# Edge network of a two-layer graph kernel: rows made unique over a pair of tiles, the pair's accumulating scatters issued back to back

## The chip, the cores and the metric

The kernel runs on one core of a Trainium2 chip, in one launch. The metric is the device time of that launch in microseconds (us), as the median of several runs. Engines are named as in the profile: PE is TensorE (PEld its weight loads), DVE is VectorE, ACT is ScalarE, POOL is GpSimd, SP is SyncE.

## What is computed

50000 nodes with 256 features, 50000 edges (`src`, `dst`, sorted by `dst`). A graph attention layer and a layer norm come first; then the edge network, which the change touches; then a last layer norm. Cut to the edge network:

```python
h = jnp.concatenate([n_embed[senders], n_embed[receivers]], axis=-1)   # senders = src
h = jnp.tanh(h @ W0 + b0)
h = jnp.tanh(h @ W1 + b1)
h = h @ W2 + b2
h = h * (e_embed @ Wg)
m = _segment_mean(h, senders, n)
out = _layernorm(x + m)
```

`segment_mean` adds the edge rows that have the same sender and divides by their count.

## The kernel before, in words

The kernel is a sequence of stages. The stage before the edge network writes two tables to HBM: PA (406 columns of the receiver or sender half of `h @ W0`, with the reciprocal count beside it, 408 columns in all) and PB (the other half), and the array x, which is `out_x`. The edge network (from L1269 on) then takes the edges in 98 groups of four tiles of 128 edges, and two groups' buffers alternate (index `s`). The last stage (L1656 on) is the layer norm over `out_x`.

What each engine does for group g of the edge network:

- POOL `gather` (L1311): two indirect DMAs per tile bring 128 rows of PA and of PB into `u_pa` and `u_pb`; eight per group. `scatter` (L1324): one indirect DMA per tile adds the 128 summed rows in `u_sums` to `out_x` in HBM at the rows in `u_row`; four per group. Rows out of bounds are dropped. `body` (L1340) gathers group g+2 and scatters group g-2 in turns. A scatter waits until the evacuation of its half group and its row numbers are there, and until all earlier scatters have landed (`need(pool, o_st, 16 * (4 * g + j))`, L1328), since two tiles can hold the same sender and an accumulating DMA reads, adds and writes.
- DVE `add` (L1550): waits for the eight gathers, copies the reciprocal counts (L1554) and adds PA to PB (L1555, L1559). `low0`, `low1`, `edge_low`, `low_message` make the low parts of numbers that are split in two for the f32r products. `message` multiplies layer 2 by the gate. `select` (L1584) builds for each tile the 128x128 matrix that sums rows of equal key inside the tile into the first of them, and counts in `u_first` how many of the rows up to itself have a row's key; `scatter_rows` (L1593) moves rows that are not the first beyond the bound.
- PE: `transposes` of the summed rows for group g+1, `layer1`, `gate`, `layer2` of group g, `combine` (L1414: the selection times the high and the low message, a pair of tiles per half of one PSUM bank), `spread` (the keys as a row for `select`).
- ACT: tanh twice per product (`hidden0`, `hidden1`), `gated`, `high_message`, and `sums` (L1502), which evacuates the bank of `combine` to `u_sums`.

Each engine runs its own list in program order, written out by hand; semaphores tie them. In its body for group g the DVE ends with `add(g + 2)`, and the body for g+1 begins with `select(g)`. In the PE's body for group g+1 the first thing behind `layer1(g+1, 0)` is `transposes(g+2, 0)`, which needs that `add`.

```python
def free(g):                       # POOL, ahead of a group's gathers
    pool.wait_ge(v_ix, g + 1)
    need(pool, v_sum, g - 1)
    need(pool, p_t, 4 * (g - 1))
```

Where the kernel's last two groups have no gathers beside them, POOL issues scatters alone: 16 of them, behind the last one that had gathers ahead of it.

## Time and profile before

| | us |
|---|---|
| median of three runs (lowest, highest) | 6148.02 (6139.2, 6167.52) |
| the profiled execution, its own time | 6160.46 |
| its span in the trace | 6158.8 |
| the edge network's POOL instructions, first to last start | 3787.04 to 5831.44 |
| busy in the span: PE, DVE, ACT, POOL | 4460.0 (72%), 3805.1 (62%), 2758.8 (45%), 3465.6 (56%) |

The page cuts the span into 40 slices of 154 us. The edge network fills the slices from the 25th to the 38th; the last one or two belong to the layer norm. In these slices PE and POOL both show seven or eight tenths, the DVE and ACT six, the DMA engines five. A line of the timeline gives the start, the duration, the engine and the source line, and in brackets how long the engine had stood idle before and what ended that: "issue" means that nothing shown in the profile was waited for.

### The profile page before, as it was taken

What the parts mean: (1) busy time and instruction counts of PE and PEld (TensorE: products, weight loads), DVE (VectorE), ACT (ScalarE), POOL (GpSimd) and SP (SyncE); (2) the same over time, 40 slices, a digit from 0 to 9 for tenths busy, and PEclk for the clock granted to TensorE, in tenths of its full rate; (3) what the DMA queues carried; (4) which work ended last, traced back from release to release, by engine and by line L of the source; (5) the groups of instructions that cost most, each with busy time, mean ns of one, the idle gap of its engine ahead of it and who ended that gap; (6) DMA issues with size and microseconds to landing.
All of it is one profiled execution on the core that took longest, in us unless ns stands there. A gap on an engine that the chain in (4) does not pass through costs nothing. (4 is left out here: it accounts for less than half of the span.)

```text
span 6158.8 us, 98689 instructions
## 1 busy us (share of the span) xinstructions
PE 4460.0 (72%) x23300; PEld 3492.5 (57%) x23300; DVE 3805.1 (62%) x12481; ACT 2758.8 (45%) x6177; POOL 3465.6 (56%) x3119
## 2 busy tenths in 40 slices
PE   7998555555555556649999997888888888888500
PEld 6776222222222334439999996777777777777400
DVE  5666555555554455559898985665656656565364
ACT  1222222222222233326666664666666666666365
POOL 1112555555555566645555554777777777777422
PEclk9999666666676677779999998999999999999755
DMA  5664000000000655559999996555555555555397
GB/s 163 201 201 133 7 6 6 6 6 6 6 7 5 145 158 169 158 156 365 356 370 359 368 355 219 122 121 122 122 120 119 123 121 120 120 122 121 58 376 290
DMA packets 721257, 940.50 MB, mean 153 GB/s; under 512 B 179231, under 2 KB 632856, under 8 KB 708704
## 3 DMA queue, kind: packets, MB, share of 16 engines
q0 software_dynamic: 183840, 376.08, 27.1%
q10 hardware_dynamic: 216893, 321.19, 14.5%
q1 hardware_dynamic: 320471, 242.66, 12.3%
q8 instruction: 16, 0.26, 0.0%
q14 instruction: 37, 0.30, 0.0%
HBM read 514.78 MB, written 425.15 MB: 153 GB/s over the span
## 5 line engine op out<-in xcount | busy, mean ns | idle before, releaser
L1189 PE MATMUL bank<-w0r,n_x1T 128*128 128x406 f32 x4704 | 903.8, 351 | 34.2 <-ACT n_pa L1237 18.4
L1189 PEld LDWEIGHTS bank<-w0r,n_x1T 128*128 128x128 f32 x4704 | 868.9, 189 | 57.8 <-ACT n_pa L1237 40.2
L1330 POOL DMA_INDIRECT out_x<-u_sums,u_row x392 | 673.3, 1718 | 238.9 <-issue 178.1
L576 PE MATMUL bank<-table,ohloT 128*128 128x392 f32 x784 | 484.8, 710 | 412.2 <-issue 208.3
L1383 PE MATMUL bank<-u_h,w1r 128*108 128x512 f32 (+1 forms) x2646 | 749.5, 432 | 0.0
L520 POOL DMA_INDIRECT DS<-by_dst,rank_int x392 | 387.9, 990 | 540.1 <-DVE by_dst L635 427.3
L1383 PEld LDWEIGHTS bank<-u_h,w1r 128*108 128x108 f32 (+1 forms) x2646 | 476.2, 187 | 144.9
L681 POOL DMA_INDIRECT xg<-XP,m_src x392 | 415.1, 1059 | 246.3 <-DVE m_src L697 126.1
L1065 POOL DMA_INDIRECT n_cg<-CT,n_last x392 | 445.3, 1136 | 177.0 <-issue 95.1
L1313 POOL DMA_INDIRECT u_pa<-PA,u_rows x392 | 441.1, 1125 | 170.5 <-issue 103.9
L1313 POOL DMA_INDIRECT u_pb<-PB,u_rows x392 | 436.1, 1113 | 119.5 <-issue 119.5
L1383 PE MATMUL bank<-w2r,u_h 108*128 108x256 f32 x3528 | 480.8, 281 | 0.2 <-DVE u_h L1574 0.2
L576 PEld LDWEIGHTS bank<-table,ohloT 128*128 128x128 f32 x784 | 167.4, 251 | 552.2 <-ACT ohloT L550 295.2
L621 DVE CUSTOM_DVE_ANT_0 found<-bank,ohhi,earlier 128x392 f32<-128x392 f32 x392 | 242.9, 620 | 382.5 <-remote 293.0
L1371 PE MATMUL bank<-ident,u_pb 128*128 128x128 f32 (+1 forms) x1568 | 258.6, 291 | 265.5 <-DVE u_pb L1559 264.9
L528 POOL DMA_INDIRECT r_sgather<-XP,r_dst x392 | 378.9, 967 | 126.3 <-issue 118.2
L1383 PEld LDWEIGHTS bank<-w2r,u_h 108*128 108x128 f32 x3528 | 444.2, 188 | 0.4 <-DVE u_h L1574 0.4
L784 PE MATMUL bank<-msg,m_sel 128*128 128x260 f32 x784 | 272.0, 506 | 208.4 <-DVE msg L731 170.9
L550 ACT CAST ohloT<-bank 128x128 f32<-128x128 f16 x392 | 104.4, 266 | 676.0 <-remote 408.3
L1371 PEld LDWEIGHTS bank<-ident,u_pb 128*128 128x128 f32 (+1 forms) x1568 | 195.8, 144 | 342.2 <-issue 163.2
L328 DVE TENSOR_SCALAR ohhi<-iota,key_hi 128x392 f16<-128x392 f16 x1176 | 381.7, 325 | 1.0 <-issue 1.0
L1475 ACT ACTIVATE u_tanh_k<-bank,b0s 128x512 f32<-128x512 f32 (+1 forms) x392 | 272.1, 694 | 223.5 <-PE bank L1371 211.6
(258 smaller groups left out, 10221.4 us busy)
## 6 DMA issues: line engine op xcount, KB each, us to landing
PA<-n_pa ACTq DMA_DIRECT2D x98, 816.0 KB
PB<-n_pb ACTq DMA_DIRECT2D x98, 812.0 KB
XP<-xps POOLq DMA_DIRECT2D x98, 528.0 KB, 4.1
CT<-ct ACTq DMA_DIRECT2D x98, 528.0 KB
n_xp<-XP SPq DMA_DIRECT2D x98, 528.0 KB
xin<-in_x SPq DMA_DIRECT2D x97, 512.0 KB, 4.9
n_x<-in_x SPq DMA_DIRECT2D x97, 512.0 KB
out_x<-n_x ACTq DMA_DIRECT2D x97, 512.0 KB, 5.1
```

The costliest lines, as they stand in the source:

```text
L328: o = nc.vector.tensor_scalar(ohhi[q][s][:, j, :], iota[:, 0:NT], HI[q][:, t], None, ALU.is_equal)
L520: pool.indirect_dma_start(out=DS, out_offset=bass.IndirectOffsetOnAxis(ap=ri[s][:, j:j + 1], axis=0), in_=pd[s][:, j, :], in_offset=None). ...
L528: pool.indirect_dma_start(out=sg[s][:, j, :], out_offset=None, in_=XP, element_offset=D + HEADS, in_offset=bass.IndirectOffsetOnAxis(ap=ix ...
L576: nc.tensor.matmul(B[ub[b]][:, 0:NT], oT[b][:], tab[b][:], start=True, stop=True)\
L681: pool.indirect_dma_start(out=xg[r][:, j, :], out_offset=None, in_=XP, in_offset=bass.IndirectOffsetOnAxis(ap=sr[r][:, j:j + 1], axis=0))\
L1065: pool.indirect_dma_start(out=cg[s][:, j, :], out_offset=None, in_=CT, in_offset=bass.IndirectOffsetOnAxis(ap=il[s][:, j:j + 1], axis=0)). ...
L1189: o = nc.tensor.matmul(acc, xT[s][p][:, k, e], w0r[q][:, 2 * half + k, :], start=(n == 0), stop=(n == len(terms) - 1))
L1313: pool.indirect_dma_start(out=buf[s][:, j, 0:w], out_offset=None, in_=table, in_offset=bass.IndirectOffsetOnAxis(ap=ix[s][:, 1 - q, j:j + ...
L1330: pool.indirect_dma_start(out=out, out_offset=bass.IndirectOffsetOnAxis(ap=si[s][:, j:j + 1], axis=0), in_=yo[s][:, j, :], in_offset=None, ...
L1371: o = nc.tensor.transpose(TB[k % 2][0:n, j * P:(j + 1) * P], pb[s][:, j, a:a + n], ident[:])
L1383: o = nc.tensor.matmul(acc, a[p], b[q], start=(start and n == 0), stop=(stop and n == 2))
L1475: nc.scalar.activation(thk[k % 2][0:n, :], TB[k % 2][0:n, :], ACT.Tanh, bias=b0s[0:n, k:k + 1])
```

## The change

The four tiles of a group become two pairs. Within a pair (a, b) the selection is built over both tiles: tile a's matrix now also gets the rows of b that have the same key as a row of a, and a row of b counts as the first of its key only if neither a nor the rows of b before it hold the key. So the two tiles of a pair never add to the same row.

- `select`: for each pair one operation of 128x128 as before (tile a) and one of 128x256 (the keys of a and b against those of b), with the new constant `u_prior` (ones beside the triangle `upto`), set up once before the first group.
- `combine`: six products per pair where there were four: a with a, and b into a (accumulated), and b with b.
- `scatter` waits for the landing of earlier scatters only at the even tile.
- POOL's body issues four gathers, then the pair's two scatters, and so again.

```diff
-            sel = alloc(ph, "u_sel", [P, G, P], f32r)
+            sel = alloc(ph, "u_sel", [P, G // 2, 3, P], f32r)
+            prior = alloc(ph, "u_prior", [P, 2 * P])
...
-                        need(pool, o_st, 16 * (4 * g + j))
+                        if j % 2 == 0:
+                            need(pool, o_st, 16 * (4 * g + j))
...
-                        for j in range(G):
-                            if not late(g, 2):
-                                gather(s, j)
-                            if not early(g, 2):
-                                scatter(g - 2, s, j)
+                        for h in range(G // 2):
+                            for j in (2 * h, 2 * h + 1):
+                                if not late(g, 2):
+                                    gather(s, j)
+                            for j in (2 * h, 2 * h + 1):
+                                if not early(g, 2):
+                                    scatter(g - 2, s, j)
...
-                        for j in (2 * h, 2 * h + 1):
-                            acc = CB[:, (j % 2) * D:(j % 2 + 1) * D]
-                            for q in range(2):
-                                o = nc.tensor.matmul(acc, sel[:, j, :], mg[s][q][:, j, :], start=(q == 0), stop=(q == 1))
+                        a, b = 2 * h, 2 * h + 1
+                        terms = [(0, 0, a, q) for q in range(2)] + [(0, 1, b, q) for q in range(2)]
+                        terms += [(1, 2, b, q) for q in range(2)]
+                        for n, (k, m, j, q) in enumerate(terms):
+                            o = nc.tensor.matmul(CB[:, k * D:(k + 1) * D], sel[:, h, m, :], mg[s][q][:, j, :],
+                                                 start=(n in (0, 4)), stop=(n in (3, 5)))
...
+                    c.did(nc.vector.memset(prior[:, 0:P], 1.0))
+                    c.did(nc.vector.tensor_copy(prior[:, P:2 * P], upto[:]))
...
-                        for j in range(G):
-                            o = nc.vector.scalar_tensor_tensor(sel[:, j, :], TB[1][:, j * P:(j + 1) * P], kf[s][:, j:j + 1],
-                                                               upto[:], ALU.is_equal, ALU.mult, accum_out=cnt[s][:, j:j + 1])
+                        for h in range(G // 2):
+                            a, b = 2 * h, 2 * h + 1
+                            nc.vector.scalar_tensor_tensor(sel[:, h, 0, :], TB[1][:, a * P:b * P], kf[s][:, a:a + 1],
+                                                           upto[:], ALU.is_equal, ALU.mult, accum_out=cnt[s][:, a:a + 1])
+                            o = nc.vector.scalar_tensor_tensor(sel[:, h, 1:3, :].rearrange("p m n -> p (m n)"),
+                                                               TB[1][:, a * P:(b + 1) * P], kf[s][:, b:b + 1], prior[:],
+                                                               ALU.is_equal, ALU.mult, accum_out=cnt[s][:, b:b + 1])
```

POOL's list before, one body ahead of the loop, with the semaphores that an instruction waits for. `u_out_added` counts landed scatters, `u_evacuated` is the evacuation by ACT, `u_transposed` and `u_sum` say that a group's buffers are free again:

```order
L1313 DMA u_pa<-PA,u_rows 128x408 [waits u_transposed,u_rows,u_sum]
L1313 DMA u_pb<-PB,u_rows 128x406
L1330 DMA out_x<-u_sums,u_row 50000x256 [waits u_out_added,u_evacuated,u_scatter_rows]
L1313 DMA u_pa<-PA,u_rows 128x408
L1313 DMA u_pb<-PB,u_rows 128x406
L1330 DMA out_x<-u_sums,u_row 50000x256 [waits u_out_added,u_evacuated,u_scatter_rows]
```

The same body after the change; the line numbers have moved by one or two:

```order
L1314 DMA u_pa<-PA,u_rows 128x408 [waits u_transposed,u_rows,u_sum]
L1314 DMA u_pb<-PB,u_rows 128x406
L1314 DMA u_pa<-PA,u_rows 128x408
L1314 DMA u_pb<-PB,u_rows 128x406
L1332 DMA out_x<-u_sums,u_row 50000x256 [waits u_out_added,u_evacuated,u_scatter_rows]
L1332 DMA out_x<-u_sums,u_row 50000x256 [waits u_evacuated,u_scatter_rows]
```

Two gathers and a scatter, four times, have become four gathers and two scatters, twice; the second scatter of a pair no longer waits for `u_out_added`.

The DVE's list around `select` before, from the end of one body to the first low parts of the next:

```order
L1554 COPY u_rc<-u_pa 128x4 [waits u_gate,u_gathered0]
L1555 TENSOR_TENSOR u_pb<-u_pb,u_pa 128x4x3x22
L1559 TENSOR_TENSOR u_pb<-u_pb,u_pa 128x4x384
L1589 SCALAR_TENSOR_TENSOR u_sel,u_first<-bank,u_key,upto 128x128 [waits u_combined,u_keys_spread]
L1589 SCALAR_TENSOR_TENSOR u_sel,u_first<-bank,u_key,upto 128x128 x3
L1574 TENSOR_TENSOR u_h<-u_tanh_m,u_h 108x512 [waits u_tanh_m]
```

and after:

```order
L1562 COPY u_rc<-u_pa 128x4 [waits u_gate,u_gathered0]
L1563 TENSOR_TENSOR u_pb<-u_pb,u_pa 128x4x3x22
L1567 TENSOR_TENSOR u_pb<-u_pb,u_pa 128x4x384
L1598 SCALAR_TENSOR_TENSOR u_sel,u_first<-bank,u_key,upto 128x128 [waits u_combined,u_keys_spread]
L1600 SCALAR_TENSOR_TENSOR u_sel,u_first<-bank,u_key,u_prior 128x256
L1598 SCALAR_TENSOR_TENSOR u_sel,u_first<-bank,u_key,upto 128x128
L1600 SCALAR_TENSOR_TENSOR u_sel,u_first<-bank,u_key,u_prior 128x256
L1582 TENSOR_TENSOR u_h<-u_tanh_m,u_h 108x512 [waits u_tanh_m]
```

The number of operations is the same; every second one is twice as wide.

## Rows read from the trace of the kernel before

**Rows 1.** Timeline of POOL, first gather of the first body with scatters. Columns: start us, us, engine, line, operation, tiles, count, idle before.
```profile
3848.44 0.95 POOL L1313 DMA_INDIRECT u_pa<-PA,u_rows  x1 [11.38 <-PE bank L1371]
```

**Rows 2.** Groups of POOL, 4000 to 5500 us: count | busy us, mean ns | idle before.
```profile
L1330 POOL DMA_INDIRECT out_x<-u_sums,u_row x296 | 509.4, 1721 | 148.3 <-issue 142.1 <-DMA out_x<-u_sums,u_row 6.3
L1313 POOL DMA_INDIRECT u_pa<-PA,u_rows x296 | 331.9, 1121 | 90.2 <-issue 78.9 <-DVE u_row L1599 8.2 <-ACT u_sums L1506 3.1
L1313 POOL DMA_INDIRECT u_pb<-PB,u_rows x296 | 331.7, 1121 | 90.2 <-issue 90.2
```

**Rows 3.** Timeline of POOL, the turn from one group to the next.
```profile
4510.85 0.99 POOL L1313 DMA_INDIRECT u_pa<-PA,u_rows  x1 [0.30 <-ACT u_sums L1506]
4512.14 1.05 POOL L1313 DMA_INDIRECT u_pb<-PB,u_rows  x1 [0.30 <-issue]
4513.91 1.71 POOL L1330 DMA_INDIRECT out_x<-u_sums,u_row  x1 [0.72 <-issue]
4515.92 2.54 POOL L1313 DMA_INDIRECT u_pa<-PA,u_rows  x1 [0.31 <-issue]
4518.77 1.35 POOL L1313 DMA_INDIRECT u_pb<-PB,u_rows  x1 [0.30 <-issue]
```

**Rows 4.** Timeline of DVE, the same turn and two operations ahead of it.
```profile
4511.59 0.42 DVE L1604 TENSOR_TENSOR u_message<-bank,u_gate 128x256 f32<-128x256 f32 x1
4511.93 0.42 DVE L1608 TENSOR_TENSOR u_msg<-u_message,u_msg 128x256 fp32r<-128x256 f32 x1
...
4515.43 0.17 DVE L1554 COPY u_rc<-u_pa 128x4 f32<-128x4 f32 x1 [0.75 <-DMA u_pb<-PB,u_rows]
4515.86 1.75 DVE L1559 TENSOR_TENSOR u_pb<-u_pb,u_pa 128x1536 f32<-128x1536 f32 x1
4517.52 0.34 DVE L1589 SCALAR_TENSOR_TENSOR u_sel<-bank,u_key,upto 128x128 fp32r<-128x128 f32 x1
4518.61 0.69 DVE L1574 TENSOR_TENSOR u_h<-u_tanh_m,u_h 108x512 fp32r<-108x512 f32 x1
4520.41 0.21 DVE L1598 TENSOR_SCALAR u_first<-u_first 128x4 f32<-128x4 f32 x1
```

**Rows 5.** Timeline of PE, the same turn, and the `combine` ahead of it.
```profile
4504.25 0.71 PE L1422 MATMUL bank<-u_msg,u_sel 128*128 128x256 f32 x4
4504.80 0.60 PE L1371 MATMUL bank<-ident,u_pb 128*86 128x128 f32 x4
...
4517.66 0.66 PE L1371 MATMUL bank<-ident,u_pb 128*128 128x128 f32 x4 [2.41 <-DVE u_pb L1559]
4518.07 3.69 PE L1383 MATMUL bank<-u_h,w1r 128*108 128x512 f32 x9
```

**Rows 6.** Waits from 4000 to 5500 us: total us, times, longest.
```profile
PE bank L1371 <- DVE u_pb L1559: 186.3, 74, 4.7
...
DVE u_rc L1554 <- DMA u_pb<-PB,u_rows: 80.0, 42, 3.4
```

**Rows 7.** Timeline of PE early in the stage, where the DVE does not wait for gathers.
```profile
3913.58 0.66 PE L1371 MATMUL bank<-ident,u_pb 128*128 128x128 f32 x4 [1.33 <-DVE u_pb L1559]
...
3931.94 0.65 PE L1371 MATMUL bank<-ident,u_pb 128*128 128x128 f32 x4 [1.49 <-DVE u_pb L1559]
3932.35 2.33 PE L1383 MATMUL bank<-u_h,w1r 128*108 128x512 f32 x9
```

**Rows 8.** A stretch: us, busy of PE, PEld, DVE, ACT, POOL, PEclk, DMA share, GB/s.
```profile
4074.90:4078.00 3.10, 3.10 (x10) 2.22 (x9) 1.83 (x7) 1.27 (x2) 2.58 (x2) 0.50 0.37 74
```

**Rows 9.** Timeline of POOL, the end of the stage: no gathers any more from 5754.68 on.
```profile
5754.68 1.71 POOL L1330 DMA_INDIRECT out_x<-u_sums,u_row  x1 [0.61 <-issue]
5759.56 1.57 POOL L1330 DMA_INDIRECT out_x<-u_sums,u_row  x1 [3.16 <-DMA out_x<-u_sums,u_row]
...
5831.44 1.55 POOL L1330 DMA_INDIRECT out_x<-u_sums,u_row  x1 [2.93 <-DMA out_x<-u_sums,u_row]
```

**Rows 10.** DMA queues from 5800 to 5830 us, where only scatters run.
```profile
q0 software_dynamic: 1004, 0.87, 26.2%
```

## The prediction

> **What bounds the kernel now.** I read the page's slices first: the edge network is the longest stage and its POOL and PE rows are equally high, so shares decide nothing. The groups of POOL inside the steady stretch come next. In 1500 us POOL issued 296 scatters of 1.721 us and 592 gathers of 1.121 us; its idle time was 148.3 us ahead of the scatters and 180.4 us ahead of the gathers [rows 2]. That adds up to 1501.8 us: POOL is never without work. The reader is to see what the idle time is. A gather costs 90.2 / 296 = 0.305 us of it, always, which is the gap between any two of these instructions. A scatter has 148.3 / 296 = 0.501 us, so 0.196 us more. That excess is the wait for the scatter before to land: where scatters run alone, the next one starts 3.17 us after the end of the one before (5754.68 + 1.71 to 5759.56) [rows 9], and two undisturbed gathers with three gaps are only 0.99 + 1.05 + 0.91 = 2.95 us [rows 3].
>
> A group is 296 / 4 = 74 to the 1500 us, 20.3 us; over the whole stage it is the same, (5756.4 - 3848.4) / 94 = 20.30 us for the 94 bodies that have gathers and scatters [rows 1, 9]. Written out: 8 x (1.121 + 0.305) + 4 x (1.721 + 0.501) = 20.3.
>
> PE is the follower. It waits 186.3 / 74 = 2.5 us per group for the DVE's addition, and the DVE waits 80.0 / 74 = 1.08 us per group for the gathers to land [rows 6]. How fast the chain of PE, ACT and DVE could go by itself is seen early in the stage, where the DVE does not wait for gathers: from one transposition to the next 18.36 us, with 1.3 to 1.5 us of waiting in front of it [rows 7]. So there are two clocks: POOL at 20.3 us and the compute chain at 18.4 us.
>
> **POOL's holds.** In the turn between two groups a gather took 2.54 us instead of 0.99 [rows 3]. It started at 4515.92, just behind the DVE's long addition (4515.86 to 4517.61) [rows 4], and ended 0.85 us after it: it was held until the addition was over. The next one started inside the DVE's low part (4518.61 to 4519.30) [rows 4] and took 1.35 us. Undisturbed a gather is 0.97 us and a scatter 1.62 [rows 3], so the means of rows 2 hold 8 x 0.15 + 4 x 0.10 = 1.6 us per group of such holds.
> The Trainium skill, "SBUF — State Buffer", section "Who interferes with whom", says that one of the DVE and GpSimd takes the shared port pair for a whole instruction and the other blocks, but it adds, marked as inferred, that a tensor_tensor takes only the read interface while descriptor generation needs the write interface. By that addition these holds would be zero and POOL's group 18.7 us today; the rows show 20.3, so here the measurement decides, and POOL's starts are held by tensor_tensor operations whose inputs both lie in SBUF.
>
> **The change part by part.**
> - The wait between scatters. The odd scatter waits for nothing but POOL itself; the even one for a scatter whose issue ended four gathers earlier, 5 x 0.305 + 4 x 0.97 = 5.4 us, against 3.17 us to land [rows 9]. Both waits go: 4 x 0.196 = 0.78 us per group. 20.30 becomes 19.5 us.
> - The holds. Counted from the end of a group's last gather (4513.19), the DVE resumed at +2.24 and its long addition began at +2.67 [rows 3, 4]. Before, one scatter lay between and the next gather started at +2.73, into the addition. Now two scatters follow: the second starts at +0.31 + 1.62 + 0.31 = +2.24, ahead of the addition, and runs until +3.9; the next gather starts at +4.2 and the addition ends at +4.4. So of the hold of 1.55 us some 0.2 remains where the phases are as in this turn. Where the DVE comes later (it sometimes has no wait for gathers), the first gather is held by up to 1.2 us. Bounds: the holds fall from 1.6 to some 0.9 us, or rise by 0.4. I take a fall of 0.3, nearer to no change than to the one favourable turn: POOL at 19.2 us.
> - PE. Two more products per pair. Four took 4504.25 to 4504.80, 0.14 us each [rows 5], so 4 x 0.14 = 0.55 us per group, wholly on the compute chain, which becomes 18.36 + 0.55 = 18.9 us. It lies beside POOL as long as POOL needs more than that. This is the floor of the change.
> - DVE. The four selections take 4517.52 to 4518.61, 0.27 us each. A product of 128x256 out of PSUM takes 0.34 us from start to start (4511.59 to 4511.93) [rows 4]. So a selection twice as wide adds between 0.34 - 0.27 = 0.07 and, if all of it goes by width, 0.27 us; two of them per group 0.14 to 0.54 us. I take 0.27. While they run, PE is in nine products of layer 1 that need nothing of them (4518.07 to 4521.76) [rows 5], so they are covered, and if that cover goes they cost their 0.27 us on the chain.
> - The two setup operations on the DVE run once, before the first gathers have landed: nothing.
> - The end. After the last gathers 16 more scatters ran, until 5831.44 + 1.55 = 5832.99, 76.6 us behind 5756.39 [rows 9]. Now they are 8 pairs of 1.55 + 0.31 + 1.55 + 3.17 = 6.6 us; the last ends 8 x 6.6 = 52.6 us behind. That is 24 us less. Behind the last gathers the compute chain has two groups left, 2 x 18.9 = 38 us, and the seventh pair wants the last group's sums at 3.2 + 6 x 6.6 = 43 us; so POOL stays the limit there.
>
> Sum: 94 x (20.3 - 19.2) = 103 us, and 24 us at the end: 127 us. From the profiled execution's 6160.5 that is 6033; the median of the runs lies 12.4 us lower than that execution, so the prediction against the median is **6021 us**.
>
> **Rivals.**
> 1. The compute chain becomes the bound. If the holds fall to 0.9 us, POOL would go at 18.8 us and the chain's 18.9 decides. The DVE's waits for gathers then vanish, and POOL waits ahead of a group's first gather for the transpositions. 94 x 1.4 + 24 = 156: 5992 us. For it speaks the phase above; against it, that the phase of one turn is not that of all. Chance 0.27.
> 2. The holds stay or grow: POOL at 19.5 to 19.9 us, 94 x 0.8 or 0.4, with the end 99 or 62 us: 6049 to 6086 us. Chance 0.2 (in most of it still over 0.5% faster, which is 31 us, about what a measurement of this kernel can tell from no change).
> 3. The PE's clock takes the gain back. Behind its long waits the granted clock was 0.50, that is 1.2 of 2.4 GHz [rows 8], and the nine products of layer 1 took 3.69 us instead of 2.33 [rows 5, 7], 1.36 us. A chain of 18.9 + 1.4 = 20.3 us would leave only the end: 6124 us. Against it: once the chain is late, PE's wait is down to 1.3 to 1.5 us, and behind such a wait the products took 2.33 [rows 7]; so the lower clock cannot hold in every group. Chance 0.07.
> 4. Slower: the pair lands late. Two accumulating scatters in a row could take the engines so long that the second lands well beyond 3.17 us. POOL's next pair waits once it exceeds the 5.4 us of cover, two times per group, and each microsecond beyond costs 2 us in a group. Nothing is gained any more at about 5.4 + (0.78 + 0.26) / 2 = 5.9 us, and at 6.3, two landings one after the other, it is 94 x (19.5 + 1.8 - 20.3) = 94 us slower in the bodies and nothing saved at the end: 6242 us. Already from about 6 us the DVE too would stand at `scatter_rows` (4520.41, that is +7.2) [rows 4], with low parts queued behind it that PE needs. Against it: the scatters running alone filled 26.2% of the DMA engines at one per 4.7 us [rows 10], 1.2 us each, less than the 1.92 us that POOL needs for the next. Chance 0.06.
>
> **How the numbers follow.** Forecast (POOL at 19.1 to 19.4) 0.4, rivals 1 to 4 as given. The range takes in the first three up to the top of rival 2 and leaves out rivals 3 and 4 and a rest at the low edge: 5980 to 6085 us. Faster by over 0.5% is the forecast, rival 1 and nearly all of rival 2: 0.86. Within 0.5% is rival 3 and the edge of 2: 0.08. Slower is rival 4: 0.06.
>
> **What would show it.** Idle ahead of both scatters of a pair 0.30 to 0.31 us in the steady stretch; the mean of a gather below 1.121 us and few gathers above 2 us; six products per half group in `combine`; the DVE's wait for gathers clearly below 1.08 us per group, and PE's below 2.5. Rival 1 shows as POOL idle behind PE at the first gather of groups, and no DVE wait for DMA; rival 3 as layer 1 at 3.3 to 4.2 us in most groups; rival 4 as POOL idle "by DMA out_x" at even scatters. I am wrong if POOL still stands idle longer than 0.31 us at scatters, if the second scatter's own duration exceeds 1.7 us on the mean, or if PE's waits grow.

## The result and the profile after

Where it was first measured, the changed kernel took 6293.7 us (median of four runs, 6279.8 to 6310.6) and the kernel before 6150.2 us (four runs here, three in the table of before): ratio 1.0232, 95% interval 1.0196 to 1.0268. It is **slower by 2.3%**; that it is slower is clear of the noise, that it is so by more than 2% just isn't. The prediction (6021 us, 5980 to 6085) missed it in size and in sign. The profiled execution has a span of 6278.1 us at a mean granted clock of 0.835 (before: 6158.8 and 0.844).

The experiments ran later and mostly on other chips, and this can't be left out: the kernel before takes 5636 to 5655 us on four of them (numbers 5, 7, 14 and 9) and 6210 us on a fifth (number 6), which behaves as the first one did. The first chip's number isn't on record, so it may be number 6 itself. On chip 7 the changed kernel is **faster by 3.2%**. The rest of this text is about what lies between the two results. Ratios below are always taken on one chip; times per group are also compared across the four chips of 5650 us, on which the kernel before agrees within 0.4%.

The groups of POOL in the changed kernel on the first chip, 4000 to 5500 us (count | busy us, mean ns | idle before), which answer to [rows 2]:

```profile
L1332 POOL DMA_INDIRECT out_x<-u_sums,u_row x274 | 457.5, 1670 | 83.5 <-issue 82.9 <-DVE u_rows L1556 0.6
L1314 POOL DMA_INDIRECT u_pa<-PA,u_rows x275 | 347.1, 1262 | 248.4 <-PE bank L1375 172.1 <-issue 76.3
L1314 POOL DMA_INDIRECT u_pb<-PB,u_rows x275 | 279.9, 1018 | 85.0 <-issue 74.4 <-DMA out_x<-u_sums,u_row 10.1 <-DVE u_rows L1556 0.6
```

The wait that the change takes away is gone: 83.5 / 274 = 0.305 us ahead of a scatter, the bare gap, instead of 0.501. But a group is now 4 x 1500 / 274 = 21.9 us, and POOL stands 172.1 us behind PE's transpositions, of which [rows 2] have nothing. The waits of the same stretch (us in total, times, longest), which answer to [rows 6]:

```profile
PE bank L1375 <- DVE u_pb L1567: 195.7, 68, 4.5
ACT u_gate L1500 <- PE bank L1387: 177.9, 121, 2.9
POOL u_pa L1314 <- PE bank L1375: 172.1, 46, 5.9
...
ACT u_gate L1500 <- remote: 48.0, 21, 3.1
```

PE waits 195.7 / 68 = 2.9 us each time for VectorE's addition, no less than before, and a releaser stands here that the same stretch of the kernel before does not have: "remote", a wait that ended with no instruction of this core. The timeline of the same kernel shows what it looks like (start us, us, engine, line, operation, tiles, count, idle before):

```profile
4543.75 1.23 PE L1387 MATMUL bank<-w2r,u_h 108*128 108x256 f32 x9
...
4545.48 1.22 PE L1387 MATMUL bank<-w2r,u_h 108*128 108x256 f32 x9
4545.58 1.67 POOL L1332 DMA_INDIRECT out_x<-u_sums,u_row  x1 [0.30 <-issue]
...
4546.53 0.60 PE L1435 MATMUL bank<-ident,u_key 128*128 128x128 f32 x4
4546.89 2.31 PE L1387 MATMUL bank<-u_h,w1r 128*108 128x512 f32 x9
4547.55 1.58 POOL L1332 DMA_INDIRECT out_x<-u_sums,u_row  x1 [0.30 <-issue]
4548.34 0.48 ACT L1500 ACTIVATE u_gate<-bank,u_rc 128x256 f32<-128x256 f32 x1 [3.05 <-remote]
...
4553.24 1.11 PE L1375 MATMUL bank<-ident,u_pb 128*128 128x128 f32 x4 [3.80 <-DVE u_pb L1567]
4554.01 4.19 PE L1387 MATMUL bank<-u_h,w1r 128*108 128x512 f32 x9
```

PE's layer 2 of tile 2 ended at 4544.98, and ScalarE's gate, whose other condition (the message of tile 0) was long met, began at 4548.34: by the trace the product was done 3.4 us before ScalarE could act on it. The trace models the ends of products, but PE had by then begun three later groups of products (at 4545.48, 4546.53 and 4546.89). Message, low part, the next addition all follow, PE waits 3.8 us at its end, and layer 1 behind that wait takes 4.19 us instead of 2.33 [rows 7], on the lower clock: the granted clock from 4553.3 to 4558.2 us is 0.50, which is 1.2 of 2.4 GHz.

How often this happens can be counted over the whole stage, from the starts and ends of the 392 layers 2 and the 392 gates, wherever ScalarE stood idle ahead of the gate. In the changed kernel 147 of 260 such gates began over 0.3 us after the end of their product, by up to 4.16 us and by 1.06 us on the mean of the 260. In the kernel before it is 33 of 280, by up to 1.78 and by 0.14 us on the mean. In the changed kernel on chip 7 it is none of 287, and the longest is 0.04 us. "Late" and "on time" below mean this. From ScalarE to VectorE (gate to message) and back (message to its cast) no start is more than 0.04 us behind its releaser, on the first chip as on the others, and on the four chips of 5650 us TensorE's signals aren't late either. The trace's own records of semaphores can't give these counts on the first chip: it holds 322 of the 392 signals of layer 2 there.

The changed kernel on chip 7, 3500 to 5000 us, first POOL's groups:

```profile
L1332 POOL DMA_INDIRECT out_x<-u_sums,u_row x325 | 521.9, 1606 | 99.0 <-issue 99.0
L1314 POOL DMA_INDIRECT u_pa<-PA,u_rows x325 | 357.8, 1101 | 99.1 <-issue 99.1
L1314 POOL DMA_INDIRECT u_pb<-PB,u_rows x325 | 325.7, 1002 | 99.1 <-issue 99.1
```

then one of its stretches (us, busy of PE, PEld, DVE, ACT, POOL, PEclk, DMA share, GB/s):

```profile
4000.00:4500.00 500.00, 457.77 (x3085) 397.49 (x3086) 339.24 (x847) 352.43 (x677) 400.95 (x326) 1.00 0.65 133
```

Here POOL has no wait of any kind, only gaps of 0.305 us; a group is 6000 / 325 = 18.5 us, and TensorE's granted clock is 1.00.

### The profile page after: what moved, and what is told of

Its sections match the earlier page's. It is cut to its first block and busy times, and to the rows that moved or that the text cites. A ratio compares the mean times of both kernels' runs of the same rounds, so it can differ in the third digit from the quotient of the medians.

```text
span 6278.1 us, 99187 instructions
## 1 busy us (share of the span) xinstructions
PE 4561.4 (73%) x23692; PEld 3588.4 (57%) x23692; DVE 3833.3 (61%) x12483; ACT 2755.9 (44%) x6177; POOL 3460.3 (55%) x3119
## 5 line engine op out<-in xcount | busy, mean ns | idle before, releaser
L1387 PE MATMUL bank<-u_h,w1r 128*108 128x512 f32 (+1 forms) x2646 | 813.0, 460 | 0.0
L1332 POOL DMA_INDIRECT out_x<-u_sums,u_row x392 | 653.4, 1667 | 147.0 <-issue 116.1
L1314 POOL DMA_INDIRECT u_pa<-PA,u_rows x392 | 489.0, 1247 | 392.1 <-PE bank L1375 245.8
L1387 PEld LDWEIGHTS bank<-u_h,w1r 128*108 128x108 f32 (+1 forms) x2646 | 508.6, 200 | 160.5
L1314 POOL DMA_INDIRECT u_pb<-PB,u_rows x392 | 399.1, 1018 | 120.9 <-issue 106.9
L1375 PEld LDWEIGHTS bank<-ident,u_pb 128*128 128x128 f32 (+1 forms) x1568 | 210.6, 153 | 388.1 <-issue 230.6
L1582 DVE TENSOR_TENSOR u_h<-u_tanh_m,u_h 108x512 fp32r<-108x512 f32 (+1 forms) x294 | 203.3, 691 | 341.5 <-ACT u_h L1490 224.7
```

The lines of the kernel that those rows point to most:

```text
L1314: pool.indirect_dma_start(out=buf[s][:, j, 0:w], out_offset=None, in_=table, in_offset=bass.IndirectOffsetOnAxis(ap=ix[s][:, 1 - q, j:j + ...
L1332: pool.indirect_dma_start(out=out, out_offset=bass.IndirectOffsetOnAxis(ap=si[s][:, j:j + 1], axis=0), in_=yo[s][:, j, :], in_offset=None, ...
L1375: o = nc.tensor.transpose(TB[k % 2][0:n, j * P:(j + 1) * P], pb[s][:, j, a:a + n], ident[:])
L1387: o = nc.tensor.matmul(acc, a[p], b[q], start=(start and n == 0), stop=(stop and n == 2))
```

## The experiments

Time per group is 6000 / (number of scatters in 1500 us) all through, from 3500 to 5000 us on the chips of 5650 us and from 4000 to 5500 us on the other two. "The gates" are ScalarE's `gated`, which waits for PE's layer 2.

### The order and the wait apart (chip 5, kernel before 5648 us)

Gather and scatter by turns as before, with the halved waits:

```diff
-                        for h in range(G // 2):
-                            for j in (2 * h, 2 * h + 1):
-                                if not late(g, 2):
-                                    gather(s, j)
-                            for j in (2 * h, 2 * h + 1):
-                                if not early(g, 2):
-                                    scatter(g - 2, s, j)
+                        for j in range(G):
+                            if not late(g, 2):
+                                gather(s, j)
+                            if not early(g, 2):
+                                scatter(g - 2, s, j)
```

> The changed kernel with one thing put back: POOL issues gather, scatter, gather, scatter as before (two gathers, one scatter of one tile each time), the waits on the earlier scatter stay halved, selection and combination stay over the pair. Theory A (the order is what hurts: four gathers in a row on POOL delay when TensorE's results are seen by ScalarE, and the compute chain runs at 21.8 us per group): with the runs broken up the group falls to 19.2 to 19.9 us, 6030 to 6110 us in all. Theory B (the wider selection and the two more products per pair are what hurts, with TensorE's lower clock): the order changes nothing, 6270 to 6310 us.

Measured: 5565.0 us, ratio 0.9854 (0.9836 to 0.9871), 306 scatters in 1500 us, 19.6 us per group. The times that were expected here and of the next three kernels took the first chip's 6150 us for granted and are void; the times per group can be compared. 19.6 us seemed to fit theory A (the order hurts by late signals), but no signal is late on this chip, so the run doesn't bear on it.

The same edit the other way round, the pair order in the kernel before:

> The kernel before with one thing changed: POOL issues four gathers, then two scatters, each scatter still waiting for the one before it; selection and combination by the tile as before. Theory A (order hurts): the group takes 21 us or more without any added compute, 6220 to 6320 us. Theory B (added compute hurts): the second scatter of a pair now shows its full wait of some 3 us on POOL, which the gathers no longer cover, so POOL takes 4 us more per group at most if nothing absorbs it (up to 6500 us); its compute chain stays at 18.4 us. The two are told apart by where the waits are: ScalarE's gate waiting long after the end of TensorE's second layer under A, POOL without any wait for TensorE under B.

Measured: 5993.4 us, ratio 1.0612 (1.0594 to 1.0630), 23.9 us per group. Its groups of POOL:

```profile
L1330 POOL DMA_INDIRECT out_x<-u_sums,u_row x251 | 404.3, 1611 | 427.5 <-DMA out_x<-u_sums,u_row 289.4 <-DVE u_pb L1561 99.7 <-issue 38.4
```

This is theory B's arithmetic for POOL: a scatter waits 427.5 / 251 = 1.70 us on the mean, that is 0.3 for one of a pair and 3.1 for the other. That arithmetic holds whatever the added compute costs, so it doesn't show theory B itself. No gate is late. So the pair order alone, with all four waits, costs 3.6 us per group (20.3 to 23.9).

The wide selection alone, order and waits of before (`if j % 2 == 0:` taken out, and the diff above):

> The changed selection and combination over the pair alone: POOL's order and all four waits on the earlier scatter as before. Theory A: POOL still sets the pace as before, the added 0.55 us of TensorE and 0.27 us of VectorE per group are mostly hidden: 6140 to 6200 us. Theory B: 6270 to 6310 us, as the changed kernel.

Measured: 5630.2 us, ratio 0.9971 (0.9962 to 0.9981), 299 scatters, 20.1 us per group: the added products and the wider selections cost nothing here, where POOL sets the pace.

The changed kernel with `if j % 2 == 0:` alone taken out:

> The changed kernel with the wait of every second scatter put back: four gathers, two scatters, the second waits until the first has landed (about 3 us on POOL, twice a group). Theory A: the gathers still run four in a row, so it is no faster than the changed kernel: 6290 us and up, to 6500 if POOL becomes the bound again by the two waits (19.2 + 2 x 1.6 us per group is 22.4, 6340 us). Theory B: the same POOL arithmetic, so this run tells the two apart only by the gate's waits; it prices the wait itself.

Measured: 5990.7 us, ratio 1.0608 (1.0590 to 1.0626), 251 scatters, 23.9 us per group where 22.4 was expected, as `tile_pairorder` to 3 us. In this order the halved wait is worth 5.4 us per group (23.9 to 18.5), in the old order 0.5 (20.1 to 19.6).

### The changed kernel again (chip 7, kernel before 5655 us)

> The changed kernel itself, timed again beside the kernel before. What is asked: whether it is slower wherever it runs. The first measurement (6294 against 6150 us) shows ScalarE's gates starting up to 3 us after the end of the TensorE products that they wait for, put down to no instruction of the core; the four kernels timed since show none of this, and their kernel before took 5648 us. Theory A1 (the late signals are what made the changed kernel slower, and they belong to the place where it ran): where the kernel before takes 5650 us, the changed kernel has no late gates and takes 5560 to 5650 us. Theory A2 (the order of POOL's work costs time by itself, as the pair order with all waits does at 23.8 us per group): 5700 to 5990 us wherever it runs.

Measured: 5470.3 us, ratio 0.9677 (0.9657 to 0.9698). A2 falls. A1 has the direction right and misses in size: it expected 5560 to 5650 us. What the run shows is that late signals and the slower result go together; that the one makes the other is asked below. The version between, a second time:

> The changed kernel with POOL's order of before (gather, scatter by turns) and the halved waits, a second time. Where the kernel before takes 5650 us: 5565 us as the first time, 1.5% below. Where the kernel before takes 6150 us and gates start late: between 6030 and 6110 us if it is the runs of four gathers that the late signals follow, 6200 us and more if the shorter waits alone bring them.

Measured: 5563.3 us, ratio 0.9835 (0.9811 to 0.9858). The pair order is 93 us better than the order by turns once the wait inside a pair is gone. What either does where signals come late was only asked of the changed kernel.

### Lateness put in by hand (chip 14, kernel before 5636 us)

First the kernel before, for its trace:

> The kernel before itself, for its trace where it takes 5650 us. Theory L (late TensorE signals hit the changed kernel and spared the one before): the edge stage is the same as in the first trace, 20.1 to 20.4 us per group and some 76 us from the last gather to the end of the scatters, with no wait put down to anything but an instruction of this core; the 500 us lie ahead of the edge stage. Theory M (the place is simply faster): every stage is shorter, the edge stage too.

Measured: 5636.9 us, 296 scatters in 1500 us: the same 20.3 us per group as on the first chip. The first gather of the edge stage, on this chip and on the first:

```profile
3270.95 1.02 POOL L1313 DMA_INDIRECT u_pa<-PA,u_rows  x1 [33.48 <-DVE u_rows L1548]
```

```profile
3787.04 1.02 POOL L1313 DMA_INDIRECT u_pa<-PA,u_rows  x1 [33.53 <-DVE u_rows L1548]
```

516 of the 524 us between the two executions lie ahead of it. The waits of the kernel before on the first chip in one stretch of that part, 1200 to 1700 us, where POOL issues indirect transfers as well:

```profile
ACT ohloT L550 <- remote: 126.3, 32, 7.2
DVE found L621 <- remote: 111.9, 31, 6.0
...
ACT table L548 <- remote: 85.7, 29, 4.0
```

On chip 14 the part has no wait of that name. Theory L holds: the late signals were in the first trace before the change, mostly in another stage.

Then ScalarE is held up behind its wait for layer 2, in the changed kernel and in the one before (the new buffer `held` and its clearing are left out here; the double dose has two copies in place of one):

```diff
                         need(act, v_mf, 4 * g + j - 1)
+                        for k in range(1 if j else 0):
+                            nc.scalar.copy(held[:, 1 + 1 * (j % 2) + k, :], held[:, 0, :])
```

> The changed kernel with ScalarE held up for one copy of 128x512 (about 0.6 us) ahead of each of the gates of tiles 1 to 3, behind the wait for TensorE's layer 2: 1.8 us per group, as much as the gates waited longer in the first trace of the changed kernel. Theory L: the compute chain takes the pace from POOL and grows by most of it, 19.6 to 20.6 us per group instead of 18.5, 5570 to 5670 us. Theory N (the lateness of the gates is no cause, something else lengthened the group by 3.3 us): no more than 18.8 us per group, under 5510 us.

> The same with two such copies each, 3.6 us per group. Theory L: 21.3 to 22.6 us per group, the first measurement's 21.8, 5730 to 5860 us. Theory N: under 19.5 us per group, under 5570 us.

> The kernel before with the one copy ahead of the gates of tiles 1 to 3, 1.8 us per group. Theory L: its POOL sets 20.2 us per group and its compute chain of some 18.4 has 1.8 us of room, so nearly all of it is covered: 5640 to 5700 us, while the changed kernel with the same copies loses 100 to 200 us. If the kernel before has no such room: 5750 us and more.

Measured: `after_gate1` 5643.5 us (1.0016, 1.0006 to 1.0025), `after_gate2` 5645.7 us (1.0014, 1.0004 to 1.0023), `before_gate1` 5630.9 us (0.9993, 0.9982 to 1.0005). The changed kernel goes from 18.5 to 20.5 us per group (293 scatters) and loses all of its gain; the one before stays at 20.2 (297), its time just under the 5640 to 5700 us expected. The single dose is as theory L has it. The double dose isn't: 20.5 us lies above theory N's 19.5 and below theory L's 21.3 to 22.6. No hold-up on a chip with signals on time made the changed kernel slower than the one before by anything like 2%. The timelines of PE show why the two doses cost the same. `after_gate1`:

```profile
4512.81 0.66 PE L1376 MATMUL bank<-ident,u_pb 128*128 128x128 f32 x4 [1.78 <-DVE u_pb L1571]
4513.22 3.53 PE L1388 MATMUL bank<-u_h,w1r 128*108 128x512 f32 x9
...
4533.59 0.66 PE L1376 MATMUL bank<-ident,u_pb 128*128 128x128 f32 x4 [1.89 <-DVE u_pb L1571]
4533.99 3.79 PE L1388 MATMUL bank<-u_h,w1r 128*108 128x512 f32 x9
```

and `after_gate2`:

```profile
4516.41 0.66 PE L1376 MATMUL bank<-ident,u_pb 128*128 128x128 f32 x4 [2.46 <-DVE u_pb L1571]
4516.83 2.33 PE L1388 MATMUL bank<-u_h,w1r 128*108 128x512 f32 x9
```

with one stretch of each:

```profile
4000.00:4500.00 500.00, 451.42 (x2772) 380.87 (x2771) 305.57 (x763) 352.96 (x681) 386.28 (x293) 0.93 0.56 120
```

```profile
4000.00:4500.00 500.00, 421.54 (x2766) 360.97 (x2765) 304.92 (x763) 387.86 (x754) 384.94 (x293) 0.99 0.56 119
```

With the small dose layer 1 takes 3.4 to 3.9 us in 59 of the 67 groups that can be read there (the two shown have granted clocks of 0.61 and 0.56); with the large one it takes 2.33 in 62 of 70, and 3.2 to 3.3 in the other 8. Two different sums come to the same 20.5 us.

### The clock, and the chain by itself (chip 7, kernel before 5650 us)

Five idle products of 128x256 ahead of PE's wait for the addition keep it busy in the gap:

```diff
                         if k == 0:
-                            pe.wait_ge(v_sum, g + 1)
-                        if k == 0:
                             need(pe, v_e, g)
+                            for _ in range(5):
+                                nc.tensor.matmul(TB[0][:, 0:D], wgr[0][:, 0:P], wgr[0][:], start=True, stop=True)
+                            pe.wait_ge(v_sum, g + 1)
```

> The changed kernel with the 0.6 us copies ahead of the gates of tiles 1 to 3 (20.5 us per group, clock 0.93, 5643 us), and in addition five idle products of 128x256 on TensorE ahead of its wait for VectorE's add, where it stood still for 1.8 us per group; their result is overwritten. Theory C (most of the 2.0 us that the copies cost is TensorE at its lower clock behind that wait): the granted clock returns to 0.98 or more and the group to 18.6 to 19.3 us, 5480 to 5550 us. Theory D (the delay itself is what costs): the clock may return, the group stays at 20 us or above, 5600 us and more.

> The changed kernel with the five idle products alone. POOL sets 18.5 us per group and the clock is 1.00 already, so under both theories nothing is won: 5465 to 5480 us. If the products come in the way of the real ones (TensorE has about 1.6 us of idle time per group, they take some 1.4), up to 5530 us.

Measured: `after_gate1_fill` 5525.3 us (0.9786, 0.9762 to 0.9810) where the version without the idle products had a ratio of 1.0016; `after_fill` 5470.8 us (0.9686, 0.9663 to 0.9709), no loss. The turn in `after_gate1_fill`:

```profile
4519.28 0.75 PE L1368 MATMUL bank<-wgr 128*128 128x256 f32 x5
4521.23 0.66 PE L1377 MATMUL bank<-ident,u_pb 128*128 128x128 f32 x4 [1.20 <-DVE u_pb L1572]
4521.64 2.33 PE L1389 MATMUL bank<-u_h,w1r 128*108 128x512 f32 x9
```

Theory C holds: 19.1 us per group (314 scatters), so of the 2.0 us that the hold-up had cost, 1.4 came with the lower clock. The other 0.6 isn't the compute chain: POOL waits for nothing here either, as its first group shows, and its gathers have grown from 1.05 to (385.6 + 316.2) / 630 = 1.11 us on the mean:

```profile
L1315 POOL DMA_INDIRECT u_pa<-PA,u_rows x315 | 385.6, 1224 | 96.0 <-issue 96.0
```

So POOL sets the pace at 19.1 us as well, and the chain with the 1.9 us of copies and the full clock takes no more than that.

Then the scatters of the odd tiles are left out (with the counts that wait for them halved), so that POOL is no bound:

```diff
                     def scatter(g, s, j):
 
+                        if j % 2:
+                            return
```

> The changed kernel without the scatters of every second tile: half of the edges' sums are left out of the result, and POOL has 3.8 us less per group (about 14.7 us). What is left is the compute chain of the pair version. By the prediction's third step it takes 18.9 us per group; since the changed kernel runs at 18.5 with TensorE waiting 1.6 us per group, it must be below that: 17.5 to 18.4 us.

> The kernel before without the scatters of every second tile, again with half of the sums left out: the compute chain of the tile version. The prediction has it 0.55 us per group below the pair version (two products more per pair). If TensorE's added products stand beside another engine's work, as the equal times of the pair order with all waits at either width suggest, the two are within 0.2 us.

Measured: 165 scatters of two tiles each in 1500 us in both kernels, 18.2 us per group (5430.5 and 5433.6 us). The wait that ends last is now POOL's for PE, in the changed version:

```profile
POOL u_pa L1314 <- PE bank L1377: 221.0, 83, 2.7
```

The chain that is left is the same 18.2 us for the pair as for the tile, one run of each: the two added products per pair lie beside other work.

### Equal lateness in both (chip 9, kernel before 5646 us)

> The kernel before with two copies (1.2 us) ahead of each of the gates of tiles 1 to 3, 3.6 us per group. The changed kernel took 20.5 us per group and 5646 us with the same. Theory E (at equal lateness the two are level, since the compute chain is the same 18.2 us in both, so the first result needs more lateness in the changed kernel than in the one before): 20.3 to 21.0 us per group, 5640 to 5710 us. Theory F (the kernel before has some room of its own that the changed one lacks, so that equal lateness already makes the changed one slower): 20.1 us per group and under 5640 us.

> The version with POOL's order of before and halved waits (19.6 us per group, 5565 us), with one copy ahead of each of the gates of tiles 1 to 3. If the chain with these copies and TensorE's lower clock takes 20.5 us whatever POOL does: 20.4 to 20.6 us per group, 5625 to 5650 us. If the lower clock comes only with the changed kernel's order: 19.6 to 19.9 us per group, 5560 to 5590 us.

Measured: `before_gate2` 5673.2 us (1.0049, 1.0033 to 1.0064), 293 scatters, 20.5 us per group; `alt_even_gate1` 5647.5 us (1.0007, 0.9995 to 1.0019), 294 scatters, 20.4 us. Both come out as theory E and the first alternative had them, and none of the three versions is slower by 2% at equal lateness. That all three run at the pace of one chain isn't shown, though. In `alt_even_gate1` POOL stands 165.2 us of 1500 behind PE and in `after_gate2` 71.7, but in `before_gate2` it waits for PE almost never:

```profile
L1314 POOL DMA_INDIRECT u_pa<-PA,u_rows x293 | 356.1, 1215 | 91.5 <-issue 87.2 <-PE bank L1372 2.8 <-DVE u_row L1603 0.9
```

There POOL still sets the pace, with somewhat longer gathers, so the equal 20.5 us is in part a coincidence. What the runs do show is that equal lateness of the gates doesn't give the first result. That needs signals that are later in the changed kernel than in the one before, or late signals of other kinds beside the gates'.

### The same hold-ups on a chip with late signals (chip 6, kernel before 6210 us)

The last two kernels add a hold-up of VectorE ahead of the selection. They ran on a chip that has late signals of its own:

```diff
                         dve.wait_ge(p_m, g + 1)
+                        for k in range(2):
+                            nc.vector.tensor_tensor(held[:, 3 + k, :], held[:, 0, :], held[:, 0, :], ALU.subtract)
```

> The changed kernel with one copy (0.6 us) ahead of each of the gates of tiles 1 to 3, and VectorE held up for two subtractions of 128x512 (1.4 us) behind its wait for the spread keys. If lateness of both kinds is what made the first trace: 21.3 to 22.3 us per group at a clock of about 0.90, 5720 to 5820 us. If VectorE has room at that place: 20.5 us as without, 5645 us.

> The same two hold-ups in the kernel before (20.1 us per group and 5631 us with the gates' alone). If equal lateness brings both kernels to the pace of the same compute chain: within 0.5% of the changed kernel with the same hold-ups. If the kernel before has room of its own: under 20.6 us per group, under 5670 us.

Measured: `after_gate1_select` 6487.9 us, ratio 1.0441 (1.0406 to 1.0476), 257 scatters, 23.3 us per group; `before_gate1_select` 6226.7 us, ratio 1.0023 (1.0006 to 1.0041), 295 scatters, 20.3 us. The expectations in absolute time are void, since they assumed a kernel before of 5650 us. The comparison is not, and it was missed: expected within 0.5%, with the same hold-ups on the same chip the two are 4.2% apart, while chips 14 and 9 left them level. The copy that stands in front of the gate shows the difference in its idle time, first in the changed version, then in the one before, then in `after_gate1` on chip 14:

```profile
L1502 ACT COPY u_held<-u_held 128x512 f32<-128x512 f32 x193 | 119.9, 621 | 216.1 <-PE bank L1388 187.1 <-remote 26.8 <-issue 2.2
```

```profile
L1496 ACT COPY u_held<-u_held 128x512 f32<-128x512 f32 x223 | 138.5, 621 | 50.2 <-PE bank L1384 39.0
```

```profile
L1502 ACT COPY u_held<-u_held 128x512 f32<-128x512 f32 x222 | 138.4, 623 | 71.2 <-PE bank L1388 71.2
```

ScalarE waits for layer 2 1.12 us each time in the changed version, 0.23 in the one before and 0.32 where no signal is late. Where ScalarE stood idle ahead of the copy or the gate, 173 of 235 starts are over 0.3 us behind their product in the changed version, and 39 of 133 in the one before. The spread keys are late too: of their signals that the trace recorded 93 of 96 come over 0.1 us after the product in the changed version, 15 of 69 in the one before. The first chip had 147 of 260 and 33 of 280 gates. So **the lateness belongs to the chip that a kernel ran on, and its amount follows the kernel**: it is small with POOL's work by turns and large with the pair version. Each of the two measurements with late signals was taken at one time, so a chip can't be told from the time at which it was used; and the changed kernel without hold-ups was measured beside late signals on the first chip alone.

Since the pair order with all four waits (`pair_all`) and the order by turns with halved waits (`alt_even`) were never on such a chip, no run tells which of the two parts, the order or the missing wait, does it. The traces point to the order. Take the same starts of gates or copies and ask what POOL was issuing when the product ended. In the changed kernel on the first chip, 100 of 103 are late where that was the fourth gather in a row or the scatter behind it, 40 of 93 where it was the third gather, and 7 of 54 where it was the second. On chip 6, with the hold-ups, it is 118 of 120 (and 15 of 15 in the second scatter), 40 of 46 and 0 of 47. The kernel before never issues more than two gathers in a row; of its products that end in the first of them 0 of 68 are late on the first chip, and 32 of 202 of those that end in the second or in the scatter behind it (3 of 28 and 35 of 98 on chip 6). But the place in POOL's list goes with the tile whose product it is, so this is a sign and no test.

## Why the prediction was wrong, by its own steps

- **The wait between scatters** was right: 0.305 us ahead of each, on both kinds of chip.
- **The holds** were mis-sized, to the good side. On chip 7 a gather takes (357.8 + 325.7) / 650 = 1.05 us and a scatter 1.61, so by the undisturbed 0.97 and 1.62 the holds are 8 x 0.08 = 0.7 us per group; they fell by 0.9, not by 0.3. The long holds are gone, as in the favourable turn of [rows 3, 4]: 23 of 591 gathers take over 2 us in the kernel before on chip 14, 1 of 650 in the changed kernel on chip 7. POOL goes at 18.5 us, not at 19.2.
- **PE's 0.55 us on the chain** was wrong: it is zero (18.2 us with either width, one run each). The floor of 18.9 that rival 1 is built on does not exist.
- **The selections** were right: 0.476 us for the wide one and 0.342 for the narrow on chip 7, so 0.27 us more per group, and covered, since `alt_all` is no slower than the kernel before. What the setup costs was not taken by itself.
- **The end** was right in size, 52.6 us forecast. The last scatter of the bodies and the last of all on chip 7:

```profile
5089.07 1.58 POOL L1332 DMA_INDIRECT out_x<-u_sums,u_row  x1 [0.30 <-issue]
5093.82 1.68 POOL L1332 DMA_INDIRECT out_x<-u_sums,u_row  x1 [3.17 <-DMA out_x<-u_sums,u_row]
...
5142.13 1.55 POOL L1332 DMA_INDIRECT out_x<-u_sums,u_row  x1 [0.30 <-issue]
```

5143.68 - 5090.65 = 53.0 us. The second row also ends rival 4: a pair lands 3.17 us behind its second scatter, as a single one does. Rival 4 was the only one that had the changed kernel slower, and it wasn't the reason.

Where signals are on time the sum closes. The first gather ahead of the bodies' scatters on chip 7, and on chip 14 for the kernel before:

```profile
3345.09 0.94 POOL L1314 DMA_INDIRECT u_pa<-PA,u_rows  x1 [7.45 <-PE bank L1375]
```

```profile
3327.50 0.95 POOL L1313 DMA_INDIRECT u_pa<-PA,u_rows  x1 [7.21 <-PE bank L1371]
...
5233.56 1.62 POOL L1330 DMA_INDIRECT out_x<-u_sums,u_row  x1 [0.56 <-issue]
...
5309.07 1.55 POOL L1330 DMA_INDIRECT out_x<-u_sums,u_row  x1 [2.97 <-DMA out_x<-u_sums,u_row]
```

The bodies take (5090.65 - 3345.09) / 94 = 18.57 against (5235.18 - 3327.50) / 94 = 20.29 us, which is 162 us, and the end 53.0 against 75.4, which is 22: 184 us, and the medians on chip 7 differ by 185. The forecast was 127.

**The step that failed** stands in the first part: "the compute chain at 18.4 us", read early in the stage and taken for a property of the code. The prediction let that chain, with 0.55 us more, lie beside POOL. On the first chip the changed kernel takes 21.9 us per group, and POOL waits 2.5 us in each for the chain. Of the 3.4 us above chip 7, POOL's own instructions take 1.0 us more; the rest of the account is on the chain. The gates' longer waits make up to 4 x (235.8 / 275 - 121.2 / 324) = 1.9 us, from these rows of the first chip and of chip 7:

```profile
L1500 ACT ACTIVATE u_gate<-bank,u_rc 128x256 f32<-128x256 f32 x275 | 131.5, 478 | 235.8 <-PE bank L1387 177.9 <-remote 48.0 <-issue 9.1
```

```profile
L1500 ACT ACTIVATE u_gate<-bank,u_rc 128x256 f32<-128x256 f32 x324 | 155.4, 480 | 121.2 <-PE bank L1387 120.3
```

and layer 1 at the lower clock 1.4 to 1.9 us (3.68 and 4.19 us against 2.33). This is an estimate; the parts overlap, and late signals of the spread keys and of layer 1 are in it too. No hold-up put in by hand gave more than 20.5 us on a chip with signals on time, so how late signals come to 21.9 us is argued from the traces, and what makes them late is open. Rival 3 had the second part, with a price of 1.4 us and a chance of 0.07, and its counter-argument was wrong: "once the chain is late, PE's wait is down to 1.3 to 1.5 us". With late signals it is 2.2 to 4.5 us where layer 1 is slow (55 of the 63 groups that can be read from 4000 to 5500 us), and `after_gate1` has the lower clock behind a wait of 1.8. That the late signals would grow was in no rival. That they existed could be read: in the kernel before, from 400 to 3000 us, the waits put down to "remote" are up to 408 us in one group of instructions, and I had looked at the edge stage only.

The forecast of 6021 us would have been too cautious had all signals been on time: 185 us gained against 127, by the holds and with the chain's 0.55 us absent.

## What to carry to other kernels

Read the whole trace for waits that end with no instruction of the core, even where the change is elsewhere: here they went with signals that came late, and the change, which issues four gathers in a row and waits less, met many more of them. A chain measured while another engine sets the pace is a price for that order of work alone; here the group took 18.2, 20.5 and 21.9 us where POOL waited for the chain. When a kernel's gain is wanted on any chip, a verdict from one chip is one sample: the same two programs gave 1.023 and 0.968. Where TensorE's one long wait per group goes with its lower clock, a few idle products in the wait may give most of it back (from a ratio of 1.0016 to 0.9786 here, with 0.9677 as the undisturbed value) and cost nothing where they aren't needed.

## What was not expected of the hardware

- The same kernel doesn't take the same time everywhere. The kernel before takes 5636 to 5655 us on four chips and 6150 and 6210 in the two other measurements, 9 to 10% more. In the traces of the first chip and of chip 14 nearly all of that lies ahead of the edge stage, in a part where ScalarE and VectorE wait for TensorE's results up to 7.2 us with no instruction behind the wait. Of the signals that were looked at only TensorE's are late, and almost only while POOL issues indirect transfers. In the kernel before on the first chip, of the TensorE signals that the trace recorded, 596 of 3463 are over 0.1 us late within 2 us of such an instruction and 13 of 1098 elsewhere; on chip 14 it is none of 5572. No run takes the transfers away, so that they cause it isn't shown.
- The lower clock does not go by the length of the wait alone: in `after_gate1` layer 1 took 3.4 to 3.9 us behind waits of 1.8 to 1.9 us in 59 of 67 groups, and in `after_gate2` 2.33 us behind waits of 2.4 to 2.6 in 62 of 70. The two kernels differ by one more copy on ScalarE.
- Two accumulating scatters issued 0.3 us apart land no later than one: 3.11 to 3.23 us after the second, by the waits ahead of the last eight pairs on chip 7.
- Taking a wait away may be worth ten times more in one order than in another: 5.4 us per group with the scatters in pairs, 0.5 by turns.
